# Causal mask by a TensorE matmul, and several heads' scores under one maximum

## The reference

```
x = x + attention_a(layernorm(x))     # 16 heads of 16, with biases, no mask
x = x + ffn(layernorm(x))
x = x + attention_b(layernorm(x))     # 16 heads of 16, rotary embedding, causal mask
x = x + ffn(layernorm(x))

scores = q @ k.T / sqrt(16)           # attention_b: where(causal, scores, -1e9)
attn = softmax(scores) @ v
ffn: gate = sigmoid((x @ Wq.T) @ routers.T); leaf_prob = products of gates down a tree of 8 levels
     (leaf_prob @ leaf_values) @ Wout_w.T + Wout_b
```

## Time and profile before

| what | value |
|---|---|
| median of 3 runs | 1221.77 us (1220.28 to 1222.41) |
| profiled execution, its time | 1224.61 us |
| profiled execution, span of its instructions | 1222.9 us |
| PE busy | 1112.1 us, 91% |
| DVE busy | 927.2 us, 76% |
| ACT busy | 720.2 us, 59% |
| POOL busy | 302.7 us, 25% |
| L1082 score matmuls, x1024 | 360.3 us busy |
| L842 plain maxima, x512 | 337.1 us busy, mean 683 ns |
| L838 masked minima, x512, and their readouts, x512 | 247.7 and 72.9 us busy, mean 502 and 142 ns |
| granted TensorE clock over the span | 0.957 |

### The profile page before, as it was taken

One profiled execution on the slowest core, in us unless ns is written; L12 is line 12 of the kernel. 1 busy time (PEld: TensorE's weight loads), 2 busy tenths in 40 slices (PEclk: granted clock), 3 DMA queues, 4 the chain that ended last, 5 costly groups with the idle time before them and its releaser, 6 DMA issues.

```text
span 1222.9 us, 18868 instructions
## 1 busy us (share of the span) xinstructions
PE 1112.1 (91%) x6160; PEld 546.0 (45%) x6160; DVE 927.2 (76%) x2599; ACT 720.2 (59%) x1457; POOL 302.7 (25%) x324
## 2 busy tenths in 40 slices
PE   6589999969999998999999998999999998897986
PEld 3133353434544454444544454444544444443544
DVE  3568778657888879797898869797888867774834
ACT  3056765546647775576747774676747665554551
POOL 3011101321315022331315122331315143261210
PEclk9589999989999999999999999999989999987988
DMA  7322220131403240041403241041402212021000
GB/s 207 65 69 70 63 58 21 35 91 48 105 1 101 74 108 16 18 139 35 104 2 95 79 95 28 19 138 35 105 1 75 83 42 81 1 64 41 19 8 28
DMA packets 67121, 75.33 MB, mean 62 GB/s; under 512 B 12464, under 2 KB 52816, under 8 KB 67024
## 3 DMA queue, kind: packets, MB, share of 16 engines
q1 hardware_dynamic: 66960, 74.09, 22.6%
q0 software_dynamic: 64, 0.03, 0.0%
HBM read 12.45 MB, written 4.19 MB: 14 GB/s over the span
## 4 chain that ended last, share of the span: by engine, by line
PE 55%; DVE 25%; ACT 6%; SPq 5%; issue 4%; DMA 4%; POOL 1%; DVEq 0%; ACTq 0%; POOLq 0%
PE ps_work L1212 12%; PE ps_out L1128 11%; PE ps_max L1082 10%; PE ps_key L1104 9%; PE ps_work L1237 9%; DVE neg_max L842 7%; SPq L492 4%; DVE ps_max L838 4%; DVE scratch L996 3%; PE ps_work L1183 3%; ACT probs L750 2%; DMA q_stack<-q_part 2%; DVE scratch L968 2%; DVE scratch L999 2%; DVE moments L938 1%
## 5 line engine op out<-in xcount | busy, mean ns | idle before, releaser
L750 ACT ACTIVATE probs<-ps_key 128x512 f32<-128x512 f32 (+3 forms) x1024 | 514.4, 518 | 424.2 <-PE ps_key L1104 420.7
L1082 PE MATMUL ps_max<-k_stack,q_stack 96*128 96x512 bf16 (+3 forms) x1024 | 360.3, 355 | 58.2 <-DMA q_stack<-q_part 25.2
L842 DVE TENSOR_REDUCE neg_max<-ps_max 128x1 bf16<-128x512 f32 x512 | 337.1, 683 | 90.5 <-PE ps_max L1082 89.2
L1104 PE MATMUL ps_key<-q_stack,k_stack 97*128 97x512 bf16 (+3 forms) x1024 | 353.5, 348 | 18.6 <-ACT probs L750 12.8
L838 DVE CUSTOM_DVE_ANT_0 ps_max<-ps_max,mask_b 128x128 f32<-128x128 f32 (+3 forms) x512 | 247.7, 502 | 126.4 <-PE ps_max L1082 124.4
L1082 PEld LDWEIGHTS ps_max<-k_stack,q_stack 96*128 96x128 bf16 x1024 | 100.0, 98 | 327.0 <-DVE neg_max L842 121.3
L1128 PE MATMUL ps_out<-probs,v_ones 128*32 128x512 f32 (+3 forms) x2048 | 236.5, 535 | 0.6 <-POOL probs L655 0.6
L655 POOL TENSOR_SCALAR_AFFINE_SELECT probs<-probs 128x512 f32<-128x512 f32 x128 | 82.9, 648 | 462.8 <-ACT probs L750 462.1
L1104 PEld LDWEIGHTS ps_key<-q_stack,k_stack 97*128 97x128 bf16 x1024 | 101.3, 99 | 140.9 <-ACT probs L750 84.6
L1183 PE MATMUL ps_work<-ident,scratch 128*128 128x128 f32 x384 | 65.7, 298 | 21.5 <-DMA a_v_bias<-in_a_v_bias 9.2
L677 POOL TENSOR_TENSOR rstd<-variance,minus_half 128x4 f32<-128x4 f32 (+1 forms) x34 | 33.2, 975 | 209.2 <-DVE variance L951 177.2
(11 more groups left out here) (83 smaller groups left out, 1200.7 us busy)
## 6 DMA issues: line engine op xcount, KB each, us to landing
k_stack<-k_part SPq DMA_DIRECT2D x48, 256.0 KB
q_stack<-q_part SPq DMA_DIRECT2D x48, 256.0 KB
k_stack<-k_part SPq DMA_DIRECT2D x96, 128.0 KB
q_stack<-q_part SPq DMA_DIRECT2D x96, 128.0 KB
x_in<-in_x SPq DMA_DIRECT2D x8, 512.0 KB, 4.1
q_stack<-shift_rows SPq DMA_DIRECT2D x256, 1.0 KB, 1.7
x_again<-in_x SPq DMA_DIRECT2D x8, 512.0 KB, 4.0
x_moved<-x_plain SPq DMA_DIRECT2D x7, 512.0 KB, 3.0
```

What stands on the lines that cost most here:

```text
L750: act.activation(probs[step % RING][:, j, q0:T], ps_key[slot % 2][:, 0:T - q0], ACT.Exp, scale=SCALE).then_inc(on["exp_done"], 1)
L842: dve.tensor_reduce(out=dst, in_=src, axis=AX_X, op=ALU.max, negate=True)\
L1082: pe.matmul(dst[:, 0:keys], q_stack[n % 2][0:SPLIT_ROWS, h, P * qt:P * qt + P], k_stack[n % 2][0:SPLIT_ROWS, h, 0:keys], start=True, stop= ...
L1104: pe.matmul(ps_key[slot % 2][:, 0:T - q0], k_stack[n % 2][0:STACK_ROWS, h, P * kb:P * kb + P], q_stack[n % 2][0:STACK_ROWS, h, q0:T], star ...
```

## The change

Units of a causal phase no longer have one head each. Of 16 unit numbers in a group 11 are used: number 0 has query tile 0 of all four heads (4 x 128 keys in one bank), numbers 2 and 5 have query tile 1 of two heads each (2 x 256 keys), four have query tile 2 of one head (384 keys), four query tile 3 of one head (512 keys); at the five other numbers nothing is done. After the score matmuls of a unit PE issues one more matmul, which adds the mask to the last 128 keys of each head in the bank: stationary operand ident_b (a bf16 identity), moving operand mask_b, 128 wide and repeated for each head. DVE then takes the plain negated maximum for all units, over a view of heads x keys, with one result for each head. The banks are dealt out in turn over the units that exist, and PE always waits for the maximum three units back. mask_b shrinks from 512 to 128 columns; POOL makes ident_b at the start and two counts on `zeroed` and `constants` go up by one.

```diff
+CAUSAL_UNITS = {0: (0, (0, 1, 2, 3)), 2: (1, (0, 1)), 3: (2, (0,)), 5: (1, (2, 3)), 6: (2, (1,)), 8: (3, (0,)),
+                9: (2, (2,)), 11: (3, (1,)), 12: (2, (3,)), 14: (3, (2,)), 15: (3, (3,))}
+def tile_and_heads(n, unit):
+    if causal(n):
+        return CAUSAL_UNITS.get(unit % 16, (0, ()))
+    return unit % TILES, (unit % 16 // TILES,)
+def score_banks():
+    uses = [(n, unit) for n in range(PHASES) for unit in range(SLOTS) if tile_and_heads(n, unit)[1]]
+    return {use: at % SCORE_BANKS for at, use in enumerate(uses)}
...
-        mask_b = sb("mask_b", [P, T], BF16)
+        mask_b = sb("mask_b", [P, P], BF16)
+        ident_b = sb("ident_b", [P, P], BF16)
...
+        def by_max(bank, heads, keys):
+            return bank[:, 0:len(heads) * keys].rearrange("p (h k) -> p h k", h=len(heads))
...
+            pool.memset(ident_b[:, :], 0.0).then_inc(zeroed, 1)
+            pool.wait_ge(zeroed, 6)
+            pool.affine_select(out=ident_b[:, :], in_=ident_b[:, :], compare_op=ALU.not_equal, fill=1.0, base=0,
+                               pattern=[[-1, P]], channel_multiplier=1).then_inc(constants, 1)
...
-                    if causal(n):
-
-                        dve.tensor_tensor_reduce(out=src, in0=src, in1=mask_b[:, T - keys:], scale=-1.0,
-                                                 scalar=-MASKED, op0=ALU.add, op1=ALU.min, accum_out=dst)\
-                           .then_inc(on["max_done"], 1)
-                    else:
-                        dve.tensor_reduce(out=dst, in_=src, axis=AX_X, op=ALU.max, negate=True)\
-                           .then_inc(on["max_done"], 1)
+                    dst = neg_max[g % 2][:, TILES * heads[0] + qt:TILES * heads[-1] + qt + 1:TILES]
+                    dve.tensor_reduce(out=dst, in_=by_max(max_bank[n, unit], heads, keys), axis=AX_X, op=ALU.max,
+                                      negate=True).then_inc(on["max_done"], 1)
...
-                back = units_since(n, unit)
-                if count.some("max_done", back):
-                    pe.wait_ge(on["max_done"], count.of("max_done", back))
+                if count.some("max_done", SCORE_BANKS - 1):
+                    pe.wait_ge(on["max_done"], count.of("max_done", SCORE_BANKS - 1))
                 count.add("max_done")
-                dst = ps_max[score_bank(n, unit)]
-                pe.matmul(dst[:, 0:keys], q_stack[n % 2][0:SPLIT_ROWS, h, P * qt:P * qt + P],
-                          k_stack[n % 2][0:SPLIT_ROWS, h, 0:keys], start=True, stop=True).then_inc(on["scores_full"], 1)
+                dst = by_max(max_bank[n, unit], heads, keys)
+                for at, j in enumerate(heads):
+                    h = GROUP * g + j
+                    last = pe.matmul(dst[:, at, :], q_stack[n % 2][0:SPLIT_ROWS, h, P * qt:P * qt + P],
+                                     k_stack[n % 2][0:SPLIT_ROWS, h, 0:keys], start=(at == 0), stop=not causal(n))
+                if causal(n):
+
+                    mask = mask_b[:, :].unsqueeze(1).broadcast_to([P, len(heads), P])
+                    last = pe.matmul(dst[:, :, keys - P:keys], ident_b[:, :], mask, start=False, stop=True)
+                last.then_inc(on["scores_full"], 1)
```

More of the change, by code:

```diff
@@ L225, in score_unit @@
     n, unit = n + (slot + LEAD) // SLOTS, (slot + LEAD) % SLOTS
[L226 to L237, removed]
+    return n, unit, unit // 16
+CAUSAL_UNITS = {0: (0, (0, 1, 2, 3)), 2: (1, (0, 1)), 3: (2, (0,)), 5: (1, (2, 3)), 6: (2, (1,)), 8: (3, (0,)),
[7 more added lines that the diff above has]
+    return {use: at % SCORE_BANKS for at, use in enumerate(uses)}
 def shift_due(n, unit):
@@ L372, in build @@
         ps_work = [bank(f"ps_work{i}", [P, T]) for i in range(2)]
+        max_bank = {use: ps_max[i] for use, i in score_banks().items()}
         bank_of = {use: ps_work[i] for use, i in work_banks().items()}
+        def by_max(bank, heads, keys):
+            return bank[:, 0:len(heads) * keys].rearrange("p (h k) -> p h k", h=len(heads))
         def by_tile(bank):
@@ L469, in send_shift @@
             def send_shift(n, slot):
-                n, unit, g, _, _ = score_unit(n, slot)
+                n, unit, g = score_unit(n, slot)
                 if not shift_due(n, unit):
@@ L630, in _ @@
                 pool.memset(values_of(s)[:, :, :, DH:VALUE], 1.0).then_inc(constants, 1)
-            pool.wait_ge(zeroed, 5)
+            pool.memset(ident_b[:, :], 0.0).then_inc(zeroed, 1)
+            pool.wait_ge(zeroed, 6)
+            pool.affine_select(out=ident_b[:, :], in_=ident_b[:, :], compare_op=ALU.not_equal, fill=1.0, base=0,
+                               pattern=[[-1, P]], channel_multiplier=1).then_inc(constants, 1)
             pool.affine_select(out=ident[:, :], in_=ident[:, :], compare_op=ALU.not_equal, fill=1.0, base=0,
                                pattern=[[-1, P]], channel_multiplier=1).then_inc(constants, 1)
-            pool.affine_select(out=mask_b[:, T - P:], in_=mask_b[:, T - P:], compare_op=ALU.is_ge, fill=MASKED, base=0,
+            pool.affine_select(out=mask_b[:, :], in_=mask_b[:, :], compare_op=ALU.is_ge, fill=MASKED, base=0,
                                pattern=[[-1, P]], channel_multiplier=1).then_inc(constants, 1)
@@ L828, in _, with since @@
             count = Count()
+            def since(n, unit):
+                return sum(n < PHASES and bool(tile_and_heads(n, u)[1]) for u in range(unit - SHIFT_LAG, unit + 1))
             def largest(n, slot):
-                n, unit, g, j, qt = score_unit(n, slot)
-                if n < PHASES:
+                n, unit, g = score_unit(n, slot)
+                qt, heads = tile_and_heads(n, unit)
+                if n < PHASES and heads:
                     keys = P * (qt + 1) if causal(n) else T
                     dve.wait_ge(on["scores_full"], count.next("scores_full"))
-                    src, dst = ps_max[score_bank(n, unit)][:, 0:keys], neg_max[g % 2][:, TILES * j + qt:TILES * j + qt + 1]
-                    if causal(n):
-                        dve.tensor_tensor_reduce(out=src, in0=src, in1=mask_b[:, T - keys:], scale=-1.0,
-                                                 scalar=-MASKED, op0=ALU.add, op1=ALU.min, accum_out=dst)\
-                           .then_inc(on["max_done"], 1)
-                    else:
-                        dve.tensor_reduce(out=dst, in_=src, axis=AX_X, op=ALU.max, negate=True)\
-                           .then_inc(on["max_done"], 1)
+                    dst = neg_max[g % 2][:, TILES * heads[0] + qt:TILES * heads[-1] + qt + 1:TILES]
+                    dve.tensor_reduce(out=dst, in_=by_max(max_bank[n, unit], heads, keys), axis=AX_X, op=ALU.max,
+                                      negate=True).then_inc(on["max_done"], 1)
                     count.add("max_done")
@@ L847, in largest @@
                     sent = on["shift_sent0"] if h == 0 else on["shift_sent1"]
-                    dve.wait_ge(on["max_done"], count.of("max_done", SHIFT_LAG + 1 if n < PHASES else 0))
+                    dve.wait_ge(on["max_done"], count.of("max_done", since(n, unit)))
                     if count.some(f"shift_sent{h}"):
@@ L876, in opening @@
             def opening():
-                dve.wait_ge(constants, 6)
+                dve.wait_ge(constants, 7)
                 dve.wait_ge(fold_loaded, DMA * len(FOLD))
@@ L1063, in take, with scores @@
                 count.last_read[bank.name] = event, count.n[event]
-            pe.wait_ge(constants, 6)
+            pe.wait_ge(constants, 7)
             pe.wait_ge(first_loaded, DMA * len(FIRST))
-            def scores(n, unit, g, j, qt):
+            def scores(n, unit, g):
                 if unit == 0:
@@ L1073, in scores @@
                     pe.wait_ge(held, count.of(f"stacked{n % 2}") * DMA)
-                h = GROUP * g + j
+                qt, heads = tile_and_heads(n, unit)
+                if not heads:
+                    return
                 keys = P * (qt + 1) if causal(n) else T
-                back = units_since(n, unit)
-                if count.some("max_done", back):
-                    pe.wait_ge(on["max_done"], count.of("max_done", back))
+                if count.some("max_done", SCORE_BANKS - 1):
+                    pe.wait_ge(on["max_done"], count.of("max_done", SCORE_BANKS - 1))
                 count.add("max_done")
-                dst = ps_max[score_bank(n, unit)]
-                pe.matmul(dst[:, 0:keys], q_stack[n % 2][0:SPLIT_ROWS, h, P * qt:P * qt + P],
-                          k_stack[n % 2][0:SPLIT_ROWS, h, 0:keys], start=True, stop=True).then_inc(on["scores_full"], 1)
+                dst = by_max(max_bank[n, unit], heads, keys)
[7 more added lines that the diff above has]
+                last.then_inc(on["scores_full"], 1)
             def ahead(n, slot):
-                n, unit, g, j, qt = score_unit(n, slot)
+                n, unit, g = score_unit(n, slot)
                 if n < PHASES:
-                    scores(n, unit, g, j, qt)
```

(1 more changed line is left out.)

## The result

The changed kernel takes 1235.18 us (median of 4 runs, 1234.19 to 1238.39) against 1221.03: a ratio of 1.0125, 95% interval 1.01 to 1.015. It is slower, by 14.2 us where 7.1 were forecast. That is twice the forecast, still inside the range of 1218 to 1238 and just inside the upper end of the forecast of 1225 to 1236.

A forecast was written before the change was run, and what follows sets the result against it. The prediction took PE to bound the steady part: 30.1 us of mask matmuls, less 11 us of stalls in steady stretches and 12 in the three last, gives +7.1, 1228.9 us. Forecast 1225 to 1236, range 1218 to 1238.

The forecast's parts named there:

- What bounds the kernel: Steady masked stretches: PE is nearly full (busy 63.8 of 65.6 us in phase 9), DVE is not (51.1).
- The price of the masks: On PE in causal phases: 352 added mask matmuls cost 30.1 us, with their weight loads hidden.
- rival (d): Mask matmuls on PE: their weight loads are exposed, +42 us, 1264 us; chance 0.03.
- DVE's side: Causal maxima on DVE: 512 instructions become 352, a group 6.6 to 6.1 us, 15 us of DVE time in all.
- The share of the waits that goes: PE's stalls in masked stretches: 11 us recovered in five steady ones, 12 us in the three last.
- The 1 us each for ACT and for the landing of the stack: Three last stretches: 1 us less waiting for ACT, 1 us of mask work hidden before the query stack lands.
- The slack of the banks: Three score banks span about 4.4 slots instead of 3, so DVE may lag one slot (about 1.1 us) more.
- (c): Masked stretches: stalls on maxima become PE waits for the exponential, about 10 us recovered, +20, 1242 us; chance 0.09.
- (a): Masked stretches: DVE relief wins, over 30 us recovered, -5 us, 1217 us; chance 0.15.
- (b): Whole kernel: mask cost and relief cancel, 28 to 32 us recovered, say 1222 us; chance 0.17.
- The sum: Whole kernel: 30.1 - 11 - 12 = +7.1 us, the median going from 1221.8 to 1228.9 us.
- the 208 within 2 us: Sign of being right: the three last masked stretches together stay within 2 us of 208 us.

The follow-up runs named there:

- e4: The changed kernel with each mask matmul issued twice; 1255.19 us, ratio 1.0289 to the kernel before.
- e9: The kernel before with a 128-column mask matmul added to each causal unit, DVE's own masked minimum kept; 1236.40 us, ratio 1.0124.
- e1: The changed kernel without its 352 mask matmuls, units still grouped, maximum taken over masked keys too; 1215.05 us, ratio 0.9957 to the kernel before.
- e2: The changed kernel without mask matmuls and with one head per causal unit again; 1217.26 us, ratio 0.9977 to the kernel before.
- e3: The changed kernel with its mask matmuls but one head per causal unit, so no grouping; 1233.36 us, ratio 1.0108 to the kernel before.

## Why the prediction came out as it did

**What bounds the kernel: right.** PE's column work sets the steady stretches. e4 and e9 show it: 3.6 us more of it lengthen them by 2.1 to 3.1 us, while the same relief of DVE (busy 51.1 to 46.3 us) alone, in e1, shortens them by 0.9.

**The price of the masks: right.** 30.1 us forecast, 29.0 by the spacings (256 columns take 0.111 us and not the 0.12 read from the earlier trace rows). The loads stayed hidden, so rival (d) fell: 227 of the 256 narrow masks are followed within 0.060 us, although their rows overlap those of the running matmul and each load prints 0.10 us. Behind the other 29 stands a key matmul that starts later, by up to 1.15 us; where the trace names who it waited for, that is mostly ACT.

The Trainium skill, "TensorE: Matmul & The Clock Gate", section "The mechanism", states that a weight load overlaps a running matmul only when their row groups differ. These masks contradict that sentence. The same section also lets a load run ahead when it goes to a background weight buffer, and that fits them.

**DVE's side: right in size.** 512 maxima became 352 in causal phases. DVE's printed busy time fell by 36 us in the kernel, more than the 15 us forecast, since the print of a masked minimum holds more that runs beside the next instruction. By the distances of starts in dense places the forecast stands: 0.60 us for 512 columns and 0.46 for 384, hence 6.1 us a group. By form in the changed kernel, maxima with two and four results cost what one with 512 columns does:

```profile
L854 DVE TENSOR_REDUCE neg_max<-ps_max 128x1 bf16<-128x512 f32 x640 | 424.7, 686 | 153.8 <-PE ps_max L1097 88.7 <-PE ps_max L1102 63.3
L854 DVE TENSOR_REDUCE neg_max<-ps_max 128x1 bf16<-128x384 f32 x128 | 70.6, 552 | 14.7 <-PE ps_max L1102 14.3
L854 DVE TENSOR_REDUCE neg_max<-ps_max 128x2 bf16<-128x512 f32 x64 | 44.2, 691 | 63.9 <-PE ps_max L1102 63.9
L854 DVE TENSOR_REDUCE neg_max<-ps_max 128x4 bf16<-128x512 f32 x32 | 22.2, 693 | 36.3 <-PE ps_max L1102 36.3
```

**The share of the waits that goes: this step failed in size.** I had 23 us of 30 beside other work, 11 in the steady part and 12 in the three last stretches. It was 5 x 3.6 - 9.1 = 8.9 and 3 x 3.6 - 3.2 = 7.6 us, 16.5 together, and about 2.7 of the 7.6 is clock. In the steady part the stalls on maxima went as forecast (1.2 us to none), but the value bias of L1045 kept three quarters of its 0.8 us (0.6), and ACT's waits, of which 0.3 us should have gone, went up by 0.9 with the relief (e1) and down by 0.7 to 0.9 with the masks, a sum near nothing. In the three last stretches I took 10 us of the 15.3 us behind DVE. They became 8.8, 6.5 less, of which a part is mask work that fills and no relief, and the rest moved: maxima 11.5 to 0.9, other work of DVE 3.8 to 7.9. The 1 us each for ACT and for the landing of the stack did not come: waits for ACT went from 8.3 to 8.7, the list's wait for the stack from 9.0 to 10.2. The trace shows how. The kernel before, DVE from the sum of a tile to the second half of its normalization:

```profile
1155.65 0.69 DVE L900 TENSOR_TENSOR x_causal<-ps_work,x_moved 128x512 f32<-128x512 f32 x1
...
1160.68 0.73 DVE L968 TENSOR_SCALAR scratch<-x_causal,spread,rstd 128x256 f32<-128x256 f32 x2
```

and the changed one, with the transposes that wait on PE behind it:

```profile
1169.30 0.68 DVE L912 TENSOR_TENSOR x_causal<-ps_work,x_moved 128x512 f32<-128x512 f32 x1
...
1174.30 0.73 DVE L980 TENSOR_SCALAR scratch<-x_causal,spread,rstd 128x256 f32<-128x256 f32 x2
```

```profile
1173.84 0.66 PE L1203 MATMUL ps_work<-ident,scratch 128*128 128x128 f32 x4 [0.47 <-DVE scratch L980]
...
1175.08 0.66 PE L1203 MATMUL ps_work<-ident,scratch 128*128 128x128 f32 x4 [0.25 <-DVE scratch L980]
```

5.03 us before, 5.00 after: the chain is as long as it was, because DVE works almost without a pause either way and has hardly less to do in it. Before, PE stopped ahead of score matmuls on the way there; now the banks let it pass, and it stops at the end of the chain. The slack of the banks, which I had priced at about a slot, moved the stall and did not remove it. The experiments say the same. Grouping alone, from e2 to e1, turned 8.4 us of waits for maxima into 8.6 us of others and left the length of the three last stretches at 204 us. With masks, from e3 to the changed kernel, maxima went from 8.0 to 0.9 us, other DVE from 3.5 to 7.9, ACT from 6.1 to 8.7, and the stretches did not get shorter (208.7, 210.2). The times at half clock differ within these pairs (27 us in e2 and 24 in e1, 17 in e3 and 20 in the changed kernel), so a gain or loss of 1 to 3 us in length can't be read from them; the exchange of waits can. Which stall became which is inferred from these sums; only this place and its like in phases 13 and 14 were read one by one.

**The rivals.** (c) was right in kind where there are no masks (e1: maxima 1.2 to 0, ACT 1.0 to 1.9), and what it says of ACT holds for DVE's chains with masks. Its price of +20 was too high, but the measured 14.2 lies nearer to it (5.8 us off) than to the forecast (7.1 off). (a) is out: it needed over 30 us recovered, 16.5 were, and the relief of DVE with no masks at all (e1) is worth 5.6 us in medians. (b) is out by the interval.

**The sum.** The forecast was 7.8 us for the steady stretches (5 x 3.76 - 11), -0.7 for the three last (3 x 3.76 - 12) and nothing elsewhere. The traces have 9.1, 3.2 and 1.3. So 3.9 of the 6.5 us by which the span missed it lie in the three last stretches, whose 210.2 us also left the 208 within 2 us that the prediction named as its sign; 1.3 lie in the steady ones, and 1.3 outside, at half clock and at the query stack of phase 2. Without the kinder clock of the three last stretches the miss would have been larger. The direction rests on the mechanism; that the time still fell into 1225 to 1236 is owed to the width of that forecast.

**A version that beats both** is e1: the mask is not needed for the maximum at all. The maximum over the whole last block of keys, masked ones included, is a valid shift as long as no masked score is so far above the others that all exponentials vanish; on these inputs the output stays right. It is 0.9957 of the kernel before and about 20 us below the changed one.

## What to carry to other kernels

Price work that is added to the fullest engine by the distance of starts, and then take half to two thirds of it as lost (16 to 20 of 29 us in this kernel), unless each stall that should hide it is named with what comes next in its place: relief of the second engine turned one owner of a stall into another here, three times (ACT, DVE's chains, maxima under two banks). More slack in buffers doesn't shorten a chain on an engine that works without pause. Before a difference of a few us between two stretches is called slack, compare their granted clock. And ask of a masked maximum whether it has to be masked: for a softmax shift it need not be, as long as the scores of one row lie close enough together.

## What was not expected of the hardware

A matmul that accumulates onto columns which its forerunner has only just streamed costs nothing extra: the mask starts 0.17 us after a 384-column score matmul, whose own spacing is 0.165 us, and the following key matmul 0.058 us later. In a run of four score matmuls of 128 columns with four weight loads, the spacing is 0.055 us. Two runs of different kernels repeat unchanged slots to 0.01 us, so differences of some tenths of a us between traces can be read slot by slot.
